# Value products of four key heads, moved from the keys' loop into the first slots of cross attention

## The reference

```python
q = (hidden_states @ q_proj_w.T).reshape(B, Q, 32, 128).transpose(0, 2, 1, 3)
k = (cross_attention_states @ k_proj_w.T).reshape(B, KV, 8, 128).transpose(0, 2, 1, 3)
v = (cross_attention_states @ v_proj_w.T).reshape(B, KV, 8, 128).transpose(0, 2, 1, 3)
q = rmsnorm(q, q_norm_w)
k = rmsnorm(jnp.repeat(k, 4, axis=1), k_norm_w)
v = jnp.repeat(v, 4, axis=1)
attn = jax.nn.softmax(jnp.einsum('bhqd,bhkd->bhqk', q, k) * scale + attention_mask, axis=-1)
out = jnp.einsum('bhqk,bhkd->bhqd', attn, v)
return out.transpose(0, 2, 1, 3).reshape(B, Q, 4096) @ o_proj_w.T
```

## Time and profile before

| | |
|---|---|
| median of 3 runs | 1085.3 us (1083.7 to 1087.15) |
| profiled execution | 1088.79 us, of which the span from the first to the last instruction is 1087.0 us |
| mean granted TensorE clock | 0.949 |
| TensorE matmuls busy | 924.5 us, 85% |
| VectorE, ScalarE, GpSimd busy | 840.0, 635.3, 688.1 us |

### The profile page before, as it was taken

The page is one execution under the profiler, slowest core; times in us unless marked ns, Lnnn a source line. Parts: engine busy times, 40 slices in busy tenths (PEclk is TensorE's granted clock), DMA queues, the critical chain, the costliest instruction groups (busy, mean ns, idle before and its releaser), DMA issues. The chain is left out here.

```text
span 1087.0 us, 21724 instructions
## 1 busy us (share of the span) xinstructions
PE 924.5 (85%) x6402; PEld 471.0 (43%) x6504; DVE 840.0 (77%) x2078; ACT 635.3 (58%) x1762; POOL 688.1 (63%) x670
## 2 busy tenths in 40 slices
PE   2389998679977799999999999998679978898567
PEld 1134454334432355555555555554234435555243
DVE  6579999438882899999999999998585746676485
ACT  3368788623432666666666766666342248888451
POOL 2659898626664677766666666674474345665393
PEclk9989999779999999999999999999889988998779
DMA  9269999934435465555655555655341258887555
GB/s 351 88 110 165 155 171 170 165 95 123 80 64 127 94 128 130 117 124 117 132 118 117 120 117 124 130 120 117 107 97 30 49 136 130 135 151 139 136 93 141
DMA packets 384003, 136.20 MB, mean 125 GB/s; under 512 B 369728, under 2 KB 370368, under 8 KB 381504
## 3 DMA queue, kind: packets, MB, share of 16 engines
q1 hardware_dynamic: 383936, 135.39, 60.3%
HBM read 42.01 MB, written 2.10 MB: 41 GB/s over the span
## 5 line engine op out<-in xcount | busy, mean ns | idle before, releaser
L157 PE MATMUL bank<-w_hi,hT 128*128 128x512 f16 (+2 forms) x1024 | 322.9, 371 | 32.9 <-PEq L350 12.5
L157 PE MATMUL bank<-w_lo,hT 128*128 128x512 bf16 (+2 forms) x469 | 171.9, 369 | 0.0
L157 PE MATMUL bank<-w_hi,small 128*128 128x512 f16 x512 | 162.8, 379 | 9.3 <-DVE small L1470 8.3
L157 PEld LDWEIGHTS bank<-w_hi,hT 128*128 128x128 f16 (+1 forms) x1024 | 100.4, 99 | 138.6 <-issue 31.9
L842 ACT ACTIVATE big<-bank,small 128x128 f32<-128x128 f32 x512 | 145.0, 385 | 21.5 <-DVE small L931 21.0
L1304 POOL TENSOR_TENSOR small<-small,mhalf 128x4 f32<-128x4 f32 x64 | 64.5, 1008 | 127.9 <-DVE small L975 127.9
L710 POOL TENSOR_TENSOR big<-big 128x512 f16<-128x512 f32 x96 | 116.7, 1222 | 34.3 <-DVE big L940 19.9
L931 DVE TENSOR_REDUCE small<-bank 128x4 f32<-128x512 f32 x128 | 86.7, 686 | 48.1 <-PE bank L758 46.9
L157 PE MATMUL bank<-small,big 128*128 128x17 f16 (+2 forms) x1728 | 106.7, 195 | 11.0 <-DMA big<-big 7.4
L1401 ACT ACTIVATE small<-small 128x128 f32<-128x128 f32 x256 | 98.8, 389 | 0.0
L157 PEld LDWEIGHTS bank<-small,big 128*128 128x128 f16 (+1 forms) x1728 | 70.7, 98 | 59.7 <-issue 15.3
(11 more groups left out here) (196 smaller groups left out, 2019.5 us busy)
## 6 DMA issues: line engine op xcount, KB each, us to landing
stage<-in_weights SPq DMA_DIRECT2D x16, 1024.0 KB, 5.3
stage<-in_weights SPq DMA_DIRECT2D x64, 256.0 KB, 2.9
big<-big SPq DMA_TRANSPOSE x168, 3.3
x<-in_x SPq DMA_DIRECT2D x2, 1024.0 KB, 6.1
big<-in_ctxT SPq DMA_DIRECT2D x1, 2048.0 KB, 16.6
big<-in_ctx SPq DMA_DIRECT2D x2, 1024.0 KB, 7.0
out<-x SPq DMA_DIRECT2D x8, 256.0 KB, 2.3
big<-in_vectors SPq DMA_DIRECT2D x5, 256.0 KB, 11.6
```

The source lines that it names most:

```text
L157: last = nc.tensor.matmul(out, lhs(a, c), rhs(b, c), start=start and n == 0, stop=stop and n == 3 * chunks - 1)
```

## The change

v_1 is taken out of `KEYS_ORDER`, with v_hi_1 and v_lo_1. `v_ready` counts one a batch. The eight products of the upper half of the value heads are issued in the fill instead, by the table `LATE_VALUES`: two ahead of slot 0 and one at the end of each of slots 0 to 5, into the two key banks, which the slots don't use. Each has its copy on ScalarE (`late_upper`) and its subtraction on VectorE (`late_lower`) at the end of the same slot in these engines' queues. TensorE waits, at the end of slot 5, until all eight are split.

```diff
--- before.py
+++ after.py
@@ -981,12 +981,15 @@
 
 
 KEYS_ORDER = {
-    "tensor": "++k_0 ++k_1 +v_0 +v_1",
-    "vector": "++k_stats_0 ++z_stats_0 ++k_stats_1 ++k_scale_0 +v_lo_0 ++k_scale_1 ++z_0 +v_lo_1",
-    "scalar": "++k_take_0 ++k_take_1 +v_hi_0 ++k_hi_0 +v_hi_1 ++k_hi_1 ++z_hi_0 +weight_hi_0",
+    "tensor": "++k_0 ++k_1 +v_0",
+    "vector": "++k_stats_0 ++z_stats_0 ++k_stats_1 ++k_scale_0 +v_lo_0 ++k_scale_1 ++z_0",
+    "scalar": "++k_take_0 ++k_take_1 +v_hi_0 ++k_hi_0 ++k_hi_1 ++z_hi_0 +weight_hi_0",
     "gpsimd": "++k_root_0 ++z_root_0 ++k_root_1 ++k_lo_0 ++k_lo_1 ++z_lo_0 +weight_lo_0",
     "sync": "++k_turn_0 ++k_turn_1 ++z_turn_0",
 }
+
+
+LATE_VALUES = {-1: (0, 1), 0: (2,), 1: (3,), 2: (4,), 3: (5,), 4: (6,), 5: (7,)}
 
 
 class CrossKeys:
@@ -1009,6 +1012,7 @@
             sem(f"keys_{n}") for n in ("k_done", "k_taken", "squares", "var", "root", "scaled", "k_hi", "k_lo"))
         self.v_done, self.v_hi, self.v_ready, self.rows_ready = (
             sem(f"keys_{n}") for n in ("v_done", "v_hi", "v_ready", "rows_ready"))
+        self.late_done, self.late_hi, self.late_ready = (sem(f"keys_{n}") for n in ("late_done", "late_hi", "late_ready"))
         self.z_stats, self.z_var, self.z_root, self.z_ready, self.z_hi, self.z_lo, self.z_turned = (
             sem(f"keys_{n}") for n in ("z_stats", "z_var", "z_root", "z_ready", "z_hi", "z_lo", "z_turned"))
         self.k_turned = [sem(f"keys_k_turned{m}") for m in range(2)]
@@ -1033,6 +1037,36 @@
                 step(what, m, it + ahead)
         for it in range(NB - far, NB):
             plain(it)
+
+    def late_values(self, slot):
+
+        return LATE_VALUES.get(slot, ())
+
+    def late_product(self, pe, slot):
+
+        for b in self.late_values(slot):
+            if b == 0:
+                pe.wait_ge(self.w_lo_dve, 2)
+                pe.wait_ge(self.w_lo_pool, 2)
+                pe.wait_ge(self.k_taken, 2 * NB)
+            after(pe, self.late_ready, b - 1)
+            product(self.nc, self.kbank[b % 2][:], context(self.chip, b), columns(self.chip.weight(self.v_slots[1])),
+                    CH).then_inc(self.late_done, 1)
+
+    def late_upper(self, act, slot):
+
+        for b in self.late_values(slot):
+            act.wait_ge(self.late_done, b + 1)
+            self.nc.scalar.activation(per_head(self.v[0], b)[:, GH:2 * GH, :], heads(self.kbank[b % 2][:]),
+                                      ACT.Copy).then_inc(self.late_hi, 1)
+
+    def late_lower(self, dve, slot):
+
+        for b in self.late_values(slot):
+            dve.wait_ge(self.late_hi, b + 1)
+            self.nc.vector.tensor_tensor(per_head(self.v[1], b)[:, GH:2 * GH, :], heads(self.kbank[b % 2][:]),
+                                         per_head(self.v[0], b)[:, GH:2 * GH, :], ALU.subtract
+                                         ).then_inc(self.late_ready, 1)
 
     def value_lo(self, eng, i, at):
 
@@ -1101,9 +1135,9 @@
                         CH).then_inc(self.k_done, 1)
             if what == "v":
                 if isinstance(b, int) and b == 0:
-                    pe.wait_ge(self.w_lo_dve, m + 1)
-                    pe.wait_ge(self.w_lo_pool, m + 1)
-                after(pe, self.v_ready, b * 2 + (m - 1))
+                    pe.wait_ge(self.w_lo_dve, 1)
+                    pe.wait_ge(self.w_lo_pool, 1)
+                after(pe, self.v_ready, b)
                 product(self.nc, self.vbank[m][:], context(self.chip, b), columns(self.chip.weight(self.v_slots[m])),
                         CH).then_inc(self.v_done, 1)
 
@@ -1127,7 +1161,7 @@
                 after(act, self.k_turned[m], b * 16)
                 nc.scalar.activation(self.khl[m][:, 0:D], self.kw[m], ACT.Copy).then_inc(self.k_hi, 1)
             if what == "v_hi":
-                act.wait_ge(self.v_done, b * 2 + (m + 1))
+                act.wait_ge(self.v_done, b + 1)
                 nc.scalar.activation(per_head(self.v[0], b)[:, m * GH:(m + 1) * GH, :], heads(self.vbank[m][:]),
                                      ACT.Copy).then_inc(self.v_hi, 1)
             if what == "z_hi":
@@ -1168,7 +1202,7 @@
                                                           op1=ALU.mult)
                 last.then_inc(self.scaled, 1)
             if what == "v_lo":
-                dve.wait_ge(self.v_hi, b * 2 + (m + 1))
+                dve.wait_ge(self.v_hi, b + 1)
                 nc.vector.tensor_tensor(per_head(self.v[1], b)[:, m * GH:(m + 1) * GH, :], heads(self.vbank[m][:]),
                                         per_head(self.v[0], b)[:, m * GH:(m + 1) * GH, :], ALU.subtract
                                         ).then_inc(self.v_ready, 1)
@@ -1243,7 +1277,7 @@
         def one(ring, bank, s, gg):
             return Use(bank, ring.tiles[bank], ring.full[bank], ring.free[bank], gg * n_slots + s + 1)
 
-        def schedule(eng, name, step):
+        def schedule(eng, name, step, beside=None):
 
 
             def slots(gg, first, end, limit):
@@ -1251,7 +1285,11 @@
                     for what, behind in CROSS_ORDER[name]:
                         if 0 <= slot - behind < limit:
                             step(what, slot - behind, gg, gg * n_slots + (slot - behind))
-
+                    if beside is not None and first == 0:
+                        beside(slot)
+
+            if beside is not None:
+                beside(-1)
             slots(0, 0, LAG, n_slots)
             with eng.Fori(0, NKV // 2 - 1) as gg:
                 slots(gg, LAG, n_slots + LAG, n_slots + LAG)
@@ -1324,6 +1362,11 @@
             def _(pe):
                 keys.tensor(pe)
 
+                def late(pe, slot):
+                    keys.late_product(pe, slot)
+                    if slot == LAG - 1:
+                        pe.wait_ge(keys.late_ready, NB)
+
                 def step(what, s, gg, k):
                     b, odd_half = s % NB, s // NB % 2
                     if what == "q":
@@ -1350,7 +1393,7 @@
                         if again(s, gg) and s == 0:
                             for turned_ in keys.k_turned:
                                 pe.wait_ge(turned_, 16 * NB)
-                            pe.wait_ge(keys.v_ready, 2 * NB)
+                            pe.wait_ge(keys.v_ready, NB)
                         key = s // NB % 2 * (NKV * NB * P) + (gg + s // n_slots) * (NB * P) + b * P
                         qT = turned(q_in, s)
                         for i in range(GH):
@@ -1376,7 +1419,7 @@
                         product(nc, a.tile[:], lambda half, c: (ah, al)[half][s % 2][:, c * P:(c + 1) * P],
                                 columns(chip.weight((even, odd)[odd_half][1])), CH).then_inc(a.full, 1)
 
-                schedule(nc.tensor, "tensor", step)
+                schedule(nc.tensor, "tensor", step, lambda slot: late(pe, slot))
 
             @block.scalar
             def _(act):
@@ -1434,7 +1477,7 @@
                         nc.scalar.activation(chip.w[0][:, incoming[m % 4], at], chip.stage[:, m % 2, at],
                                              ACT.Copy).then_inc(w_hi, 1)
 
-                schedule(nc.scalar, "scalar", step)
+                schedule(nc.scalar, "scalar", step, lambda slot: keys.late_upper(act, slot))
 
             @block.vector
             def _(dve):
@@ -1475,7 +1518,7 @@
                         at = slice((s % NB) * D, (s % NB + 1) * D)
                         nc.vector.tensor_tensor(chip.x[:, at], chip.x[:, at], a.tile[:], ALU.add).then_inc(a.free, 1)
 
-                schedule(nc.vector, "vector", step)
+                schedule(nc.vector, "vector", step, lambda slot: keys.late_lower(dve, slot))
     for i in range(2):
         chip.n_staged[i] += 64 * 2 * (NKV // 2)
```

## The result

The kernel after takes 1095.4 us (median of 17 runs, 1090.56 to 1099.95), the kernel before beside it 1087.23 us (17 runs, 1083.7 to 1092.64). The ratio is 1.0076, with an interval from 1.0059 to 1.0094: some 8.2 us slower, where I had forecast 3.6. The sign was right, the size was not, and 1095.4 lies above the range. The profiled execution has a span of 1093.6 us against 1087.0.

What follows compares the result with a forecast made beforehand. A ring of VectorE and ScalarE was taken to bound the keys' loop, TensorE the steady part from the first out product. 1085.3 + 3.1 (fill) + 0.5 (q(0) clock) = 1088.9 us, loop 0; range 1083.5 to 1092.5.

Steps and rivals of the forecast that it cites:

- The sign: Whole kernel: slower by 0.33%, with chances of 0.48 for slower, 0.41 for same and 0.11 for faster.
- the loop: Keys' loop: taking out v_1 gains 0 us; the trip stays 10.79 us and a lower clock there costs nothing.
- Rival A: Keys' loop at k_take_0: TensorE bounds it after all, up to 1.76 us gained in six trips, 1078.3 us; chance 0.11.
- rival C: TensorE's new wait or a thinned slot: the clock falls, costing 1.8 us each, 1090.7 to 1092.5 us; chance 0.12.
- the end of the loop: Last batch to q(0): q(0) starts at 333.6 as before, without idle time, and is copied 1.8 us earlier.
- the fill and the gate: Slots 0 to 5: copies' lead shrinks to 0.2 us; TensorE waits for late values, steady part 3.1 us late.
- Rival B: End of slot 5: the gate is free, only 1.0 us remains, 1086.3 us; chance 0.17.
- my own case: Loop 0 and fill 3.1 us, range 1.9 to 5.0 us slower; chance 0.60.
- The base: Starting time of the sum: 1085.3 us, the median of the runs of the kernel before.
- the 0.5 us: Added because the 1.8 us at q(0) may not be there to be gained in the runs.
- Whatever moves that start moves the end.: From the first out product on, TensorE sets the pace of some 400 us, so a later start moves the end.
- the ring: Keys' loop: VectorE's k_stats to k_scale_1, then ScalarE's k_hi_1 to k_take_0, set the 10.79 us trip, without TensorE.

Runs made afterwards that it cites:

- after_again: The changed kernel run once more, unaltered, for a second profile; its stage was 3.7 us longer than in the first profile of the changed kernel.
- weight_early: The changed kernel with ScalarE's weight_hi moved ahead of k_hi_0; loop 1.35 us shorter in all, total time that of the changed kernel.
- after_shift: The changed kernel with 160 semaphore increments in two idle times of TensorE's first stage; median 1088.97 us, ratio 1.0027 to the kernel before.
- before_padded: The kernel before with 96 semaphore increments in TensorE's queue ahead of the last v_0 of the keys' stage; stage 6.5 us longer than before.
- before_shift: The kernel before with 96 semaphore increments in two idle times of TensorE's first stage; median 1087.72 us, 0.9 us over the kernel before.
- after_padded: The changed kernel with 160 semaphore increments in TensorE's queue ahead of the last v_0; stage 17.4 us longer than in the changed kernel.
- before_weight_early: The kernel before, v_1 still in the loop, with ScalarE's weight_hi moved ahead of k_hi_0; 1082.1 us, ratio 0.9966.

## Why the prediction was wrong in size

**Right: the loop.** 0 us. The trip is 10.77 us with TensorE at 8.11. Rival A is out: its place, k_take_0, never waited for a product. The clock did fall once early in the loop, and that cost nothing, as I had reckoned. The Trainium skill's page that rival C cites (TensorE: Matmul & The Clock Gate, Why this matters for your kernels) speaks of longer gaps than 1.5 us, so I was wrong to write that the rows at 1.00 don't agree with it.

**Right: the end of the loop.** q(0) starts where it did, at full clock, and its copy is 1.81 us earlier (1.8 forecast).

**Right: the fill and the gate.** The start of the stage lay 1.87 us earlier in the profile after, so my 368.8 for the first pv and 372.7 for the first out product are 366.9 and 370.8 there; they came at 366.89 and 370.85. That the first fits so well has some luck in it: ScalarE's last late copy was 0.5 us earlier than reckoned (365.11 for 365.6), and pv(0) started 0.5 us after the subtraction's end (366.41), for which I had put nothing. The lead of the copies shrank as worked out, though to 0.59 at q(5), not 0.2. The steady part was 3.07 us late (3.1 forecast). Rival B is out: the wait was there.

**Mis-sized: the clock at the gate.** I gave rival C a chance of 0.12 and kept it out of the sum. Over three profiles of each kernel the stage went from 502.99 to 507.76 us, 4.8 us, where my own case has 3.1; the difference is mostly after_again, where the clock was low for longer ahead of q(0) and again behind the wait of 3.02 us. It may be rarer than one in three: weight_early and after_shift have the same gate, and their stages are 506.63 and 506.51 us.

**The base.** I set out from the median of three runs, 1085.3 us; over 17 runs it is 1087.23. Of the 6.5 us between 1088.9 and 1095.4, 1.9 are this.

**Unfounded: the 0.5 us** for runs in which q(0) was not slow before. In the three profiles of the kernel before, its copy comes 101.00 to 101.25 us into the stage, and it was slow each time.

**The step that failed: "Whatever moves that start moves the end."** It took the stretch behind the steady part as a fixed length that is only pushed. The range rested on it too: all its cases end at the last copy of q. But that stretch got longer itself, by 2.6 us in the mean, both over three profiles of each kernel and over seven of each block. The change makes TensorE's code longer by 96 instructions, so its instruction loads come at other places. One falls upon the transposing DMA that the chain to the end waits for, 1.6 us; that this is the code's place is shown by before_padded and before_shift, which have it without the change, and by after_padded and after_shift, which lack it with the change. The other 1.0 us isn't clear of the scatter; third x, 1.4 us late for the same reason, is one source of it.

So of the 8.2 us measured [6.4, 10.2], 3.1 are my own case and 1.6 the last turn. The profiles don't give the whole: between the means of the three pairs the stage has 4.8 us and the rest 2.6, but the kernels after began the keys' stage 2.2 us earlier, so their spans differ by 5.2 us. My reason for the sign was right; by itself it gives 3.1 us.

**What stays open.** How much of the rest's scatter (345.6 to 352.2 us, 3 us within one kernel) is the clock and how much other transfers; why a load holds up the packets on all DMA engines for over a microsecond; whether the earlier start of the stage in the three profiles of after is chance; what the shifted code gains ahead of the keys' stage; and how often the clock falls at the gate, of which so few profiles are not enough to tell. A kernel with before_weight_early's order and a chosen place of its code was not run.

## What to carry to other kernels

Before taking work off an engine, find the ring that sets the trip: here TensorE was busy for 98% of it and not in it, and a quarter of its work gone gave nothing. Work that is moved into a fill costs by the gate it needs at its end, and a gate is best put at the instruction that uses the values, not at the end of a slot; that was worth 1.65 us in the profile, and 2.9 by the ratios, whose intervals overlap.

A change of some tenths of a per cent can't be told from the place of the code: compare it with a kernel in which the old work has the new code's length, and read the traces of both, as that shift can have effects of its own (before_shift's time is that of before, though both places are as in after). And where a small gain is sought, look for the idle time on the path first: here one entry moved in ScalarE's order gave 0.34%.

## What the runs showed of the hardware that I had not expected

Loads of TensorE's instructions go over the same DMA engines as the data, 32 or 33 of 16 KB here, and one that meets a transposing DMA can stretch it: the last turn from 3.1 us to 4.4 to 4.9 us, the mean over 14 profiles from 3.2 to 4.1 us. In the drain of cross attention hardly a packet started for 1.25 us. 96 instructions more or fewer ahead of it decide which DMA is met.

A semaphore increment in TensorE's queue isn't free: in the traces of after_padded and before_padded they start 0.15 us after one another. 160 of them stretched an idle time from 7.92 to 22.72 us, 96 one from 5.02 to 12.13 us.

The length of one idle time didn't tell whether the clock falls behind it. Those of 1.95, 2.02, 2.03 and even 3.07 us (weight_early) at the gate left it at 1.00, one of 3.02 us (after_again) was followed by 0.51, and one of only 1.97 us (after_padded) by 0.50 from 382.2 us on. In the fill of before_shift an idle time of 1.48 us was followed by 0.50 from 354.7 to 358.1 us (TensorE was busy 2.44 of the 4 us up to 354); those of 1.50 and 1.56 us in the kernel before were not. The 2.44 us ahead of q(0) in the kernel before were followed by the lower level in each of three profiles.
